# Output weights split and softmax sums inverted inside the attention stage; the first expert's gate and up weights loaded inside the output stage

## The chip, the core and the metric

The kernel runs on one core of a Trainium2 chip. The metric is the device time of that core in microseconds (us), from first to last instruction. The core has five engines, each with a queue of its own: PE (TensorE, matmul), DVE (VectorE, elementwise), ACT (ScalarE, elementwise and activation functions), POOL (GpSimd) and SP (SyncE, here only a DMA issuer). Engines wait for each other by semaphores alone. DMAs are issued by SP, ACT or POOL and run beside the engines.

## What is computed

A cross attention and a layer of routed experts, all in fp32. T = 4 x 1024 tokens, H = 1024 features, 16 heads of 64, 64 experts of which each token takes 8, inner width 384.

```python
q, k, v = proj(layernorm(x), Wq, bq), proj(ctx, Wk, bk), proj(ctx, Wv, bv)
probs = softmax(where(mask, clip(q @ k.T / 8, -50, 50), -50))
ctx = probs @ v                                   # 16 heads side by side: T x 1024
delta = clip(residual_scale, 0, 0.3) * (ctx @ Wo.T + bo)
x = x + layernorm(delta) * gamma + beta
h = layernorm(x)
scores = softmax(h @ gate_weight.T)               # T x 64
topk_w, topk_idx = top_k(scores, 8); topk_w /= sum(topk_w)
y[t] = sum over the 8 experts e of t:  topk_w * ((silu(h[t] @ w_gate[e]) * (h[t] @ w_up[e])) @ w_down[e])
return x + y
```

## The kernel before, in words

The program is a row of stages. Each is a function that opens a block with a program for every engine, and none overlaps another: at a block's end each engine runs a DRAIN and meets the others at a barrier, POOL clears the stage's semaphores, and a second barrier lets the next stage begin (`Scope.clear`, L53 to L56). Between stages everything goes through tensors in HBM (`kst`, `qst`, `vst`, `ctxst`, `sums`, `rsums`, `h2st`, `table`, `dirst`). fp32 products are made from halves: a value is rounded to `hi` (ACT, a cast to fp32r), `lo` is the rest (DVE, a subtraction), and three matmuls (hi x hi, hi x lo, lo x hi) add up in PSUM.

The stages are: projections k, v and q; `attention_pass`; `reciprocal_pass`; `output_pass`; `experts_pass`.

**Attention** (L379). 4 batches of 16 heads, two heads (a pair) per loop step. A head is 8 units, one for each 128 keys, so a pair has 16 (`U`). In a unit PE makes 4 matmuls of scores for the unit three ahead (L478, L479) and 6 of values (L491 to L493). ACT takes the exponential (`exponential`, L516) and rounds it (`high`, L522); DVE clips and masks it (`clip`, L540) and makes the low half (`low`, L545), which PE waits for. Once per head DVE copies the finished context out of PSUM (`context`, L551), in the third unit of the next head. The value matmuls also make each row's softmax sum, unnormalised context and sum come out together in `att_c`. POOL stores both (L448, L451). SP loads K, Q and V of coming heads as their buffers come free.

**Reciprocals** (L586). All 4096 x 16 sums are loaded to one 128 x 512 tile, inverted by DVE (L606) and stored to `rsums`.

**Output** (L620). 32 tiles of 128 tokens. SP loads a tile of the context (`c_raw`) and of the inverses, each broadcast over a head's 64 rows (`r_t`): L702, L705. DVE multiplies them (`divide`, L909), ACT rounds (L866, L886), DVE takes the low half (`context_low`, L913), and PE multiplies with the output weights (L810 to L812, 52 matmuls per tile with the bias). At the start of the stage SP loads the 1024 x 1024 output weights in eight pieces, four buffers deep (L714), ACT and DVE split each piece (L863, L1021), and PE's first product waits for each. POOL meanwhile sets up constants, loads gamma, beta and the router's weights (`consts_in`, L774) and fills `table` (17 DMAs, L778). DVE does not divide tile 1 until `consts_in` is complete. Then come two layer norms (`normalize`), the store of x1 and h, the router (`logits_of`, `route`) and, per tile, eight indirect DMAs by POOL that scatter one (token, weight) record per token and slot to `table` (L787). DVE overwrites a record buffer only when the scatters of two tiles before have landed (L1008). At the end DVE makes a directory of the experts' tile counts and rows, which SP stores to `dirst`.

**Experts** (L1078). Per tile of 128 (token, expert) pairs: SP loads the tile's records by a row number from the directory (L1161), POOL gathers the token rows (L1200), PE transposes them (L1228), ACT and DVE split them, PE multiplies with gate and up (L1251 to L1253) and down (L1238 to L1240), ACT scales by the router's weight and POOL adds the rows to the output. The weights of the next expert are loaded by ACT's queue and split by ACT and DVE within the first tile of the expert in hand. At the start SP issues, in this order, the directory, expert 0's gate, up and down weights (1536 KB each, L1154), and then the first tile's records.

## Time and profile before

| | us |
|---|---|
| median of 3 runs | 7018.12 |
| lowest and highest run | 7014.53 and 7024.12 |
| the profiled execution | 7019.44 |
| its span, first to last instruction | 7017.9 |

| stage | from | to |
|---|---|---|
| projections | 0 | 1188 |
| attention | 1188 | 2396 |
| reciprocals | 2397 | 2405 |
| output | 2406 | 3026 |
| experts | 3026 | 7018 |

PE is busy for 6732.8 us (96% of the span), DVE for 3284.2, ACT for 3004.5 and POOL for 1123.6. The mean granted clock of TensorE is 0.98 of full speed. Times in rows are counted from the span's start. A row of a timeline begins with start and duration; in brackets behind it stands how long the engine had been idle, and what ended that. "PEld" is PE's weight load, "SPq" or "POOLq" an instruction of that engine's sequencer.

### The profile page before, as it was taken

Reading aid. Unit: us, or ns where it says so; the run is one execution under the profiler, and the core shown is the slowest. Engines: PE = TensorE matmul, PEld = TensorE weight load, DVE = VectorE, ACT = ScalarE, POOL = GpSimd, SP = SyncE. Lnnn points to the kernel's source line nnn. Section 1 sums busy time; section 2 is a strip of 40 time slices with the busy share of each in tenths; the row PEclk is TensorE's granted clock in tenths of the full one; section 3 lists DMA queues with packets and bytes.
Section 4 is the critical chain, followed back from the end, with each engine's and each line's share of the span. In section 5 each row is a group of like instructions: output and inputs, shape, how many; then the busy total and the mean of one; then the engine's idle time right before and its main releaser. Section 6 shows DMA issues by size and latency. Waiting matters only on the chain.

```text
span 7017.9 us, 104312 instructions
## 1 busy us (share of the span) xinstructions
PE 6732.8 (96%) x34594; PEld 5959.8 (85%) x34595; DVE 3284.2 (47%) x4163; ACT 3004.5 (43%) x3554; POOL 1123.6 (16%) x1037
## 2 busy tenths in 40 slices
PE   7989899999999699969999999999999999999998
PEld 6778787888888577769999999999999999999998
DVE  3433323999999688834243443332422223333333
ACT  3321222888888544424343443332422333333333
POOL 0000000000000135521111111111111111111111
PEclk9999999999999899979999999999999999999999
DMA  7663454555555477646576676664644556566565
GB/s 226 189 205 135 150 149 111 130 126 132 126 131 126 133 156 151 144 124 181 135 202 163 172 196 158 158 158 105 180 104 105 131 129 159 130 157 156 142 157 150
DMA packets 691794, 1047.60 MB, mean 149 GB/s; under 512 B 260259, under 2 KB 489636, under 8 KB 691718
## 3 DMA queue, kind: packets, MB, share of 16 engines
q0 software_dynamic: 112656, 374.28, 24.1%
q1 hardware_dynamic: 422676, 375.07, 21.5%
q10 hardware_dynamic: 156386, 297.29, 12.3%
q8 instruction: 41, 0.67, 0.0%
q14 instruction: 35, 0.29, 0.0%
HBM read 724.14 MB, written 322.31 MB: 149 GB/s over the span
## 4 chain that ended last, share of the span: by engine, by line
PE 53%; DMA 2%; issue 1%; ACT 0%; DVE 0%; ACTq 0%; SPq 0%; POOLq 0%; DVEq 0%
PE moe_ps_gate L1251 5%; PE moe_ps_gate L1253 5%; PE moe_ps_gate L1252 5%; PE moe_ps_up L1253 5%; PE moe_ps_y L1240 5%; PE moe_ps_up L1251 5%; PE moe_ps_up L1252 5%; PE moe_ps_y L1238 5%; PE moe_ps_y L1239 5%; PE moe_ps_xT L1228 3%; PE moe_ps_hT L1259 1%; DMA out<-moe_y,moe_rec_s 1%; DMA moe_rec_s<-table 1%; DVE moe_gu_lo L1344 0%; ACT moe_y L1289 0%
## 5 line engine op out<-in xcount | busy, mean ns | idle before, releaser
L1251 PE MATMUL moe_ps_gate<-moe_gu_hi,moe_xT_hi 128*128 128x384 f32 x2288 | 793.3, 347 | 24.1 <-DVE moe_gu_lo L1344 21.0
L1354 DVE TENSOR_TENSOR moe_hidden<-moe_silu,moe_ps_up 128x384 f32<-128x384 f32 x286 | 158.5, 554 | 1327.9 <-PE moe_ps_up L1253 1034.0
L1252 PE MATMUL moe_ps_gate<-moe_gu_lo,moe_xT_hi 128*128 128x384 f32 x2288 | 768.9, 336 | 0.0
L1253 PE MATMUL moe_ps_gate<-moe_gu_hi,moe_xT_lo 128*128 128x384 f32 x2288 | 768.5, 336 | 0.0
L1253 PE MATMUL moe_ps_up<-moe_gu_hi,moe_xT_lo 128*128 128x384 f32 x2288 | 765.1, 334 | 0.0
L1252 PE MATMUL moe_ps_up<-moe_gu_lo,moe_xT_hi 128*128 128x384 f32 x2288 | 764.2, 334 | 0.0
L1251 PE MATMUL moe_ps_up<-moe_gu_hi,moe_xT_hi 128*128 128x384 f32 x2288 | 764.2, 334 | 0.0
L1238 PE MATMUL moe_ps_y<-moe_d_hi,moe_hT_hi 128*128 128x512 f32 x1722 | 700.9, 407 | 1.9 <-DVE moe_hT_lo L1359 1.9
L1289 ACT ACTIVATE moe_y<-moe_ps_y,moe_rec_s 128x1024 f32<-128x1024 f32 x287 | 320.7, 1118 | 889.8 <-PE moe_ps_y L1240 514.9
L1208 POOL DMA_INDIRECT out<-moe_y,moe_rec_s x287 | 458.7, 1598 | 1418.6 <-ACT moe_y L1289 1348.2
L1240 PE MATMUL moe_ps_y<-moe_d_hi,moe_hT_lo 128*128 128x512 f32 x1722 | 678.0, 394 | 0.0
L1239 PE MATMUL moe_ps_y<-moe_d_lo,moe_hT_hi 128*128 128x512 f32 x1722 | 670.3, 389 | 0.0
L545 DVE TENSOR_TENSOR att_p_lo<-att_p,att_p_hi 128x1024 fp32r<-128x1024 f32 x512 | 626.7, 1224 | 61.6 <-ACT att_p_hi L522 55.6
L1284 ACT CAST moe_xT_hi<-moe_ps_xT 128x1024 fp32r<-128x1024 f32 x287 | 291.5, 1016 | 796.0 <-PE moe_ps_xT L1228 795.7
L522 ACT CAST att_p_hi<-att_p 128x1024 fp32r<-128x1024 f32 x512 | 539.8, 1054 | 164.3 <-PE att_ps_o L493 164.3
L1359 DVE TENSOR_TENSOR moe_hT_lo<-moe_ps_hT,moe_hT_hi 128x384 fp32r<-128x384 f32 x286 | 159.5, 558 | 931.0 <-ACT moe_hT_hi L1313 930.7
L1200 POOL DMA_INDIRECT moe_tokens<-h2st,moe_rec_g x288 | 283.3, 984 | 1824.1 <-PE moe_ps_xT L1228 1689.2
L516 ACT ACTIVATE att_e<-att_ps_sc 128x1024 f32<-128x1024 f32 x512 | 522.9, 1021 | 10.6 <-PE att_ps_sc L479 10.6
L1348 DVE TENSOR_TENSOR moe_xT_lo<-moe_ps_xT,moe_xT_hi 128x1024 fp32r<-128x1024 f32 x287 | 351.5, 1225 | 315.2 <-ACT moe_xT_hi L1284 315.2
L1251 PEld LDWEIGHTS moe_ps_gate<-moe_gu_hi,moe_xT_hi 128*128 128x128 f32 x2288 | 433.1, 189 | 26.8 <-DVE moe_gu_lo L1344 22.4
L1307 ACT ACTIVATE moe_silu<-moe_ps_gate 128x384 f32<-128x384 f32 x286 | 141.0, 493 | 693.2 <-PE moe_ps_gate L1253 401.9
L1252 PEld LDWEIGHTS moe_ps_gate<-moe_gu_lo,moe_xT_hi 128*128 128x128 f32 x2288 | 434.1, 190 | 0.0
(223 smaller groups left out, 14244.1 us busy)
## 6 DMA issues: line engine op xcount, KB each, us to landing
moe_raw_g<-in_w_gate ACTq DMA_DIRECT2D x63, 1536.0 KB, 7.1
moe_raw_u<-in_w_up ACTq DMA_DIRECT2D x63, 1536.0 KB, 12.0
moe_raw_d<-in_w_down ACTq DMA_DIRECT2D x63, 1536.0 KB, 6.8
vst<-proj_v_o SPq DMA_DIRECT2D x64, 512.0 KB, 2.6
att_kt<-kst SPq DMA_DIRECT2D x64, 512.0 KB, 3.6
att_qh<-qst SPq DMA_DIRECT2D x128, 256.0 KB, 4.7
att_ql<-qst SPq DMA_DIRECT2D x128, 256.0 KB, 5.5
att_v<-vst SPq DMA_DIRECT2D x128, 256.0 KB, 3.4
```

What stands on the lines that cost most here:

```text
L516: nc.scalar.activation(e32[:, u % 2], sc[:, u % 2], ACT.Exp, scale=1.0 / math.sqrt(HD)).then_inc(exp_done, 1)
L522: nc.scalar.copy(p_hi[:, u % 2], p32[:, u % 2]).then_inc(hi_done, 1)
L545: nc.vector.tensor_tensor(p_lo[:, u % 2], p32[:, u % 2], f32(p_hi[:, u % 2]), ALU.subtract).then_inc(lo_done, 1)
L1208: nc.gpsimd.indirect_dma_start(out=acc[:, :], out_offset=bass.IndirectOffsetOnAxis(ap=rec_s[:].bitcast(I32)[:, 0:1], axis=0), in_=y[:], in ...
L1238: nc.tensor.matmul(y_ps[:, cols], hT_hi[:, c], d_hi[:, b, c, cols], start=(c == 0), stop=False)
L1239: nc.tensor.matmul(y_ps[:, cols], hT_hi[:, c], d_lo[:, b, c, cols], start=False, stop=False)
L1240: last = nc.tensor.matmul(y_ps[:, cols], hT_lo[:, c], d_hi[:, b, c, cols], start=False, stop=(c == CI - 1))
L1251: nc.tensor.matmul(o[:, 0:I], xT_hi[:, c], gu_hi[:, b, k, c], start=(c == 0), stop=False)
L1252: nc.tensor.matmul(o[:, 0:I], xT_hi[:, c], gu_lo[:, b, k, c], start=False, stop=False)
L1253: last = nc.tensor.matmul(o[:, 0:I], xT_lo[:, c], gu_hi[:, b, k, c], start=False, stop=(c == C - 1))
L1289: nc.scalar.activation(y[:], y_ps[:], ACT.Copy, scale=rec_s[:, 1:2]).then_inc(y_done, 1)
L1348: nc.vector.tensor_tensor(xT_lo[:], xT_ps[:], f32(xT_hi[:]), ALU.subtract).then_inc(xT_lo_done, 1)
```

## The change

- **Attention.** The output weights are loaded at the start of the attention stage, right behind the loads of the first pair (L466, L467), 3 MB into a tile `raw` that the experts stage later uses for gate and up weights, and 1 MB into `w_rest`. In batch 1 (`SPLIT_AT`), whose loop over pairs is written out, ACT rounds a 128 x 256 piece in every fourth unit (`weight_high`) and DVE takes its low half two units later (`weight_low`): 32 pieces. `wo_hi` and `wo_lo` outlive the stage.
- **Context stores** move from POOL to SP (`store_context`), between SP's loads of coming heads.
- **Sums.** `sums` and `rsums` are laid out by 128-token tile. When a batch is stored, POOL loads its sums, DVE inverts them (128 x 128) in the last pair of the next batch, and POOL stores the inverses. The last batch's are inverted at the start of the output stage. `reciprocal_pass` is gone.
- **First tiles.** Near the end of attention SP loads x, context and inverses of tiles 0 and 1.
- **Output stage.** It finds the weights split. SP loads expert 0's gate and up weights there (L777). The directory stays in SBUF (`dir_sb`): the three columns are copied into it, not to HBM. The zero rows are written from a 128 x 128 tile in 16 DMAs, formerly 2. `normed` is merged into `scaled`.
- **Experts stage.** SP's first DMA is record 0, whose row is fixed (`REGION`), then the down weights. `tokens_high` and `tokens_low` of tile 0 stand between the split of gate and that of up. POOL clears one of the zero tiles, after the first gather.

```diff
 def attention_pass(...)
+                sp.dma_start(w_first, woT[0:CR * P, :].rearrange("(c p) n -> p c n", p=P)).then_inc(w_in, 16)
+                sp.dma_start(w_rest[:], woT[CR * P:H, :].rearrange("(c p) n -> p c n", p=P)).then_inc(w_in, 16)
+                def store_context(i, bt, b):
+                    sp.wait_ge(c_done, bt * NH + 2 * i + b + 1)
+                    sp.dma_start(ctxst[bass.ds((2 * i + b) * HD, HD), bt * S:(bt + 1) * S],
+                                 c32[b * HD:(b + 1) * HD, b]).then_inc(stored[b], 16)
+                    ...
+                def load(i, bt, i_before, bt_before):
+                    for b in range(2):
+                        bh = bt * NH + 2 * i + b
+                        sp.wait_ge(scores_done, (bh - 1) * C)
+                        load_scores(i, bt, b)
+                        sp.wait_ge(values_done, (bh - 1) * C)
+                        load_values(i, bt, b)
+                        store_context(i_before, bt_before, b)
+                for b in range(2):
+                    sp.dma_start(x_t[:, b], x[b * P:(b + 1) * P, :]).then_inc(first_in, 16)
+                    sp.dma_start(c_raw[:, b], ctx_v[:, :, b * P:(b + 1) * P]).then_inc(first_in, 16)
+                    for k in range(2): ...
+                        sp.dma_start(r_t[k * HD:(k + 1) * HD, b], src).then_inc(first_in, 16)
+                for b in range(2):
+                    store_context(NH // 2 - 1, B - 1, b)
 pool:
-                            pool.dma_start(ctxst[...], c32[...]).then_inc(stored[b], 16)
-                            pool.dma_start(sums[...], c32[...]).then_inc(stored[b], 16)
+                for bt in range(B - 1):
+                    for b in range(2):
+                        pool.wait_ge(stored[b], 32 * (bt + 1) * (NH // 2))
+                    pool.dma_start(sums_t[:], sums[bt * C:(bt + 1) * C]...).then_inc(sums_in, 16)
+                    pool.wait_ge(inverted, bt + 1)
+                    pool.dma_start(rsums[bt * C:(bt + 1) * C]..., rsums_t[:]).then_inc(inverses_stored, 16)
 act, in each unit u of a pair:
+                        if bt == SPLIT_AT and u % WP == 0:
+                            weight_high(i, u // WP)
 dve, in each unit u of a pair:
+                        if bt == SPLIT_AT and u % WP == 2:
+                            weight_low(i, u // WP)
+                        if bt and i == NH // 2 - 1 and u == 5:
+                            invert(bt - 1)
 def output_pass(...)
-                load_context(0, 0)
-                for c in range(C): ...
-                    sp.dma_start(w_raw[:, c % 4], woT[c * P:(c + 1) * P, :]).then_inc(w_in[c % 4], 16)
-                load_context(1, 1)
+                sp.dma_start(sums_t[:], sums[last_batch]...).then_inc(sums_in, 16)
                 sp.wait_ge(cn_done, 1)
                 load_context(2, 0)
+                sp.wait_ge(inverted, 1)
+                sp.dma_start(rsums[last_batch]..., rsums_t[:]).then_inc(inverses_stored, 16)
+                sp.wait_ge(inverses_stored, 16)
+                for raw, src in zip(raw_first, w_first):
+                    sp.dma_start(raw[:], src[0].rearrange("(c p) i -> p c i", p=P)).then_inc(raw_first_in, 16)
 pe:
-                        if first:
-                            pe.wait_ge(w_lo_done, c + 1)
 dve:
+                divide(0, 0)
+                context_low(0, 0)
+                nc.vector.reciprocal(rsums_t[:], sums_t[:]).then_inc(inverted, 1)
 def experts_pass(...)
-                sp.dma_start(dir_sb[:], dirst).then_inc(dir_in, 16)
+                sp.dma_start(rec_g[:], table[REGION:REGION + P, :]).then_inc(rec_g_in, 16)
 act (dve likewise, with tokens_low):
-                split(0, 0, 0, PIECES)
+                split(0, 0, 0, C // 2)
+                tokens_high(0)
+                split(0, 0, C // 2, PIECES)
                 load_gate_up(1)
                 load_down(1)
-                tokens_high(0)
```

How instructions move is shown at three places. The first is DVE inside attention, around the copy of a finished head's context (`att_c`). Before, in the loop over pairs:

```order
L540 TENSOR_SCALAR att_p<-att_e,att_upper 128x1024
L545 TENSOR_TENSOR att_p_lo<-att_p,att_p_hi 128x1024
L549 ISA
L550 REGISTER_ALU
L551 COPY att_c<-att_ps_o 128x1024
L537 REGISTER_ALU
L540 TENSOR_SCALAR att_p<-att_e,att_upper 128x1024
L545 TENSOR_TENSOR att_p_lo<-att_p,att_p_hi 128x1024
```

And now, in batch 1:

```order
L594 TENSOR_SCALAR att_p<-att_e,att_upper 128x1024
L599 TENSOR_TENSOR att_p_lo<-att_p,att_p_hi 128x1024
L605 COPY att_c<-att_ps_o 128x1024
L627 TENSOR_TENSOR ahead_wo_lo<-first_raw,ahead_wo_hi 128x256
L594 TENSOR_SCALAR att_p<-att_e,att_upper 128x1024
L599 TENSOR_TENSOR att_p_lo<-att_p,att_p_hi 128x1024
```

The weight piece stands directly behind the context copy, in units 2 and 10 of a pair; the pieces of units 6 and 14 stand alone.

The second is SP from the end of the attention stage into the output stage. Before (POOL stores the context, so SP has nothing to do at the end of attention):

```order
L598 DMA rec_t<-sums 128x512
L600 DMA rsums<-rec_r 128x512
L595 UNCONDITIONAL_BRANCH
L698 UNCONDITIONAL_BRANCH
L702 DMA out_c_raw<-ctxst 128x8x128
L705 DMA out_r_t<-rsums 64x8x128 x2
L714 DMA out_w_raw<-in_woT 128x1024 x8
L702 DMA out_c_raw<-ctxst 128x8x128
```

And now (`first_raw` is the tile that the expert weights use):

```order
L447 DMA ctxst<-att_c 64x1024
L450 DMA sums<-att_c 8x1x128
L423 UNCONDITIONAL_BRANCH
L743 UNCONDITIONAL_BRANCH
L758 DMA out_sums_t<-sums 128x128
L747 DMA ahead_c_raw<-ctxst 128x8x128
L750 DMA ahead_r_t<-rsums 64x8x128 x2
L762 DMA rsums<-out_rsums_t 128x128
L777 DMA first_raw<-in_w_gate 128x8x384
L777 DMA first_raw<-in_w_up 128x8x384
```

The weight loads have left the stage's start, and the last context store stands in front of the barrier on SP.

The third is SP at the start of the experts stage. Before:

```order
L1152 DMA moe_dir<-dirst 1x514
L1154 DMA moe_raw_g<-in_w_gate 128x8x384
L1154 DMA moe_raw_u<-in_w_up 128x8x384
L1154 DMA moe_raw_d<-in_w_down 128x3x1024
L1156 TENSOR_LOAD moe_dir
L1156 ISA x2
L1160 TENSOR_LOAD moe_dir
L1160 ISA x2
L1161 ISA
L1161 DMA moe_rec_g<-table 128x2
```

And now:

```order
L1189 DMA moe_rec_g<-table 128x2
L1192 DMA moe_raw_d<-in_w_down 128x3x1024
L1193 TENSOR_LOAD first_dir
```

The first record went from behind four DMAs to the front of the queue.

## Rows read from the trace of the kernel before

**Rows 1.** The page: busy tenths of PE in 40 slices of 175 us

```profile
PE   7989899999999699969999999999999999999998
```

**Rows 2.** Windows over the first handover: length, busy by engine, PEclk, DMA share, GB/s

```profile
2380.25:2405.63 25.38, 0.00 (x0) 0.00 (x0) 4.58 (x2) 0.00 (x0) 1.04 (x2) 0.55 0.11 31
2405.63:2456.01 50.38, 21.49 (x52) 13.92 (x53) 15.93 (x18) 12.62 (x13) 14.94 (x34) 0.58 0.78 254
```

**Rows 3.** Timeline from the end of attention to tile 2 of the output stage

```profile
2379.85 0.40 PE L493 MATMUL att_ps_o<-att_p_hi,att_v 128*128 128x512 f32 x1
...
2396.73 0.35 SPq L598 DMA_DIRECT2D rec_t<-sums  x1
...
2405.63 0.39 SPq L702 DMA_DIRECT2D out_c_raw<-ctxst  x1
...
2409.61 0.91 POOL L774 DMA_DIRECT2D out_gate<-in_gateT  x1
...
2424.49 1.22 DVE L909 TENSOR_TENSOR out_cn<-out_c_raw,out_r_t 128x1024 f32<-128x1024 f32 x1
...
2428.10 0.80 PE L810 MATMUL out_ps_o<-out_w_hi,out_c_hi 128*128 128x512 f32 x1 [47.85 <-DVE out_c_lo L913]
...
2433.86 0.51 PE L810 MATMUL out_ps_o<-out_w_hi,out_c_hi 128*128 128x512 f32 x1 [0.28 <-DVE out_w_lo L1021]
...
2452.33 1.23 DVE L909 TENSOR_TENSOR out_cn<-out_c_raw,out_r_t 128x1024 f32<-128x1024 f32 x1 [8.43 <-DMA out_r_t<-rsums]
...
2456.01 0.50 PE L810 MATMUL out_ps_o<-out_w_hi,out_c_hi 128*128 128x512 f32 x1 [1.61 <-DVE out_c_lo L913]
...
2471.15 1.71 PE L822 MATMUL out_ps_tps<-out_ident,out_h 128*128 128x128 f32 x8 [2.47 <-ACT out_h L892]
```

**Rows 4.** Source line L413, the attention block's end: durations in ns, start

```profile
L413 POOLq DRAIN x1: 10517/10517/10517, 2385.5 to 2385.5; - x1
```

**Rows 5.** DMA issues by line: KB each, median us to landing

```profile
ctxst<-att_c POOLq DMA_DIRECT2D x64, 256.0 KB, 2.8
out_r_t<-rsums SPq DMA_DIRECT2D x64, 256.0 KB, 12.4
out_gate<-in_gateT POOLq DMA_DIRECT2D x1, 256.0 KB, 19.8
```

**Rows 6.** Waits in attention from 1300 to 2370 us: total, times, longest

```profile
ACT att_p_hi L522 <- PE att_ps_o L493: 149.8, 463, 0.6
...
PEld att_ps_o L491 <- DVE att_p_lo L545: 21.6, 58, 0.4
```

**Rows 7.** Timeline, DVE's inversion of all sums

```profile
2399.40 3.35 DVE L606 RECIPROCAL rec_r<-rec_t 128x512 f32<-128x512 f32 x1 [17.89 <-DMA rec_t<-sums]
```

**Rows 8.** Windows, the first loads of the attention stage

```profile
1190.00:1200.00 10.00, 2.44 (x6) 1.98 (x7) 1.10 (x5) 0.35 (x1) 0.00 (x0) 0.50 1.09 259
```

**Rows 9.** Timeline of SP, the first load for the second pair

```profile
1214.22 0.36 SPq L424 DMA_DIRECT2D att_kt<-kst  x1
```

**Rows 10.** Timeline of the start of the experts stage

```profile
3026.75 0.38 SPq L1154 DMA_DIRECT2D moe_raw_g<-in_w_gate  x1
...
3031.11 31.94 SPq L1161 DMA_DIRECT2D moe_rec_g<-table  x3
...
3034.69 3.56 DVE L1344 TENSOR_TENSOR moe_gu_lo<-moe_raw_g,moe_gu_hi 128x768 fp32r<-128x768 f32 x4 [0.69 <-ACT moe_gu_hi L1280]
...
3042.79 1.01 POOL L1200 DMA_INDIRECT moe_tokens<-h2st,moe_rec_g  x1 [15.67 <-DMA moe_rec_g<-table]
...
3050.42 1.94 PE L1228 MATMUL moe_ps_xT<-moe_ident,moe_tokens 128*128 128x128 f32 x8 [47.63 <-DMA moe_tokens<-h2st,moe_rec_g]
...
3054.80 0.68 PE L1251 MATMUL moe_ps_gate<-moe_gu_hi,moe_xT_hi 128*128 128x384 f32 x1 [2.44 <-DVE moe_xT_lo L1348]
```

**Rows 11.** Source line L901, once per tile: durations in ns, first and last start

```profile
L901 ACT ACTIVATE out_d<-out_ps_o,out_rs x32: 1094/1099/1122, 2454.6 to 2974.8; 128x1024 f32<-128x1024 f32 x32
```

**Rows 12.** Waits in the output stage from 2500 to 2980 us: total, times, longest

```profile
DVE out_record L1008 <- DMA table<-out_record,out_slot: 46.2, 16, 5.0
```

More of the change, by code:

```diff
@@ L498, in _, with body @@
                     scores(0, u)
-                def body(pair, bt, next_bt, first):
+                def body(pair, bt, next_bt, first, i=None):
                     for u in range(U):
@@ L524, in _, with weight_high, body @@
                 exponential(0, 0)
-                def body(pair, bt, next_bt, first):
+                def weight_high(c, k):
+                    if c == 0 and k == 0:
+                        act.wait_ge(w_in, 32)
+                    cols = slice(k * WCOL, (k + 1) * WCOL)
+                    nc.scalar.copy(wo_hi[:, c, cols], w_raw[c][:, cols]).then_inc(w_hi_done, 1)
+                def body(pair, bt, next_bt, first, i=None):
                     for u in range(U):
@@ L1212, in _ @@
                 gather(0)
+                nc.gpsimd.memset(f32(d_lo[:, 1]), 0.0).then_inc(zeroed, 1)
                 gather(1)
```

225 lines of the change are left out of this document (112 added, 113 removed).

## Prediction

> **What bounds the kernel now.** I read the page first. PE is busy 96% of the span and sets the end; in 40 slices it shows a handful of places below 9 tenths [rows 1], of which this change touches two: 2275 to 2450 us, from attention to output, and 2975 to 3150 us, from output to experts. The windows are next [rows 2]: between 2380.25 and 2405.63 PE does nothing, and in the 50.4 us after it does 52 matmuls at a mean granted clock of 0.58. At the second place PE's idle time before its first transposes is 47.63 us [rows 10]. Everything else of the experts stage, 3963 us from 3054.80 on, is unchanged code, so what counts is how much sooner PE reaches two marks: the transposes of tile 0 at 2471.15 [rows 3], from where the output stage goes on as before, and the first gate matmul at 3054.80 [rows 10]. Then the timelines show what each waited for, and the waits in attention what the added work can disturb.
>
> **The handover to output, before.** The last value matmul starts at 2379.85 and ends at 2380.25 [rows 3]. The reciprocals' load is issued at 2396.73. Line L413 tells why so late: POOL, which stored the last context, starts its DRAIN at 2385.5 and needs 10.5 us for it [rows 4]; all others stood at the barrier. The reciprocal stage takes until 2405.63. There PE waits for context and weights until 2428.10, and its first product crawls behind the split of the weights. Product 1 waits for `divide` of tile 1 (2452.33, itself waiting for a load) and starts at 2456.01.
>
> **The same, after.** The context copy ends 1.3 us after the last matmul (2381.5; the copy took 1.22 us). SP, with no DRAIN to speak of, issues the two stores by about 2382.3; a landing of 2.8 us as on POOL's queue [rows 5] gives 2385.0. From the end of POOL's DRAIN (2396.0) to the next stage's first issue (2396.73) was 0.7 us, so the output stage begins near 2385.6, 20.0 us sooner. This needs POOL's DRAIN to be hidden. POOL's last DMA is now the store of batch 2's inverses, released in unit 5 of the last pair, ten units of 2.3 us before the end; 10.5 us fit in. The Trainium skill, VectorE: DVE Perf Modes, section The DRAIN you can't avoid, says in my words that the DRAINs of a program's frame take about 12 ns on any engine. By that rule moving the stores off POOL would bring nothing of these 10.5 us and the sum would be 6973; the trace does not agree (10,517 ns), and the row is used.
>
> In the stage, `divide` of tile 0 is first; from `divide` to the first matmul it took 3.6 us (2424.49 to 2428.10), so PE starts at 2389.2 with all weights split. The clock is at its lower level then: a mean of 0.55 over the 25.38 us of rows 2 is 0.5 with some 2.5 us at full speed, so it fell about 2.5 us after the last matmul, and 9 us pass here. The first 13 matmuls took 5.8 us before they turned short (2428.10 to 2433.86). Product 1 ran from 2456.01 to about 2468.7 (the transposes at 2471.15 had waited 2.47), 0.24 us per matmul; the other 39 take 9.4 us. Product 0 ends at 2404.4. Under it lie the last inversion, the bias's low half and the masks, each about 1 us on an engine that waits.
>
> Product 1 needs `divide` of tile 1, and DVE does not pass `consts_in` before it. POOL issues the router's weights 4.0 us into the stage (2409.61). They landed after 19.8 us [rows 5], beside 4 MB of output weights that are gone now. The nearest short transfer on that side is 2.8 us. I take 14, nearer to the row of the thing itself since gamma, beta and 17 fills stay in front or beside: `divide` at 2385.6 + 4.0 + 14 = 2403.6, and product 1 follows 3.7 us later (2452.33 to 2456.01), at 2407.3. PE has then idled 2.9 us, longer than those 2.5, so it starts cold and takes 5.8 + 9.4 = 15.2 us: the transposes stand at 2422.5. The wait for tile 2's inverses falls away, since that load starts 1 us into the stage and takes some 12.4 us [rows 5], and so does the wait of 2.47 us in front of the transposes. Gain to this mark: 2471.15 - 2422.5 = 48.6 us. Ends: consts after 2.8 us let product 1 follow product 0 warm and gain 6 more; after 19.8 us, 6 less. Expert 0's 3 MB stand on SP's queue in front of tile 3's load; at the 259 GB/s of rows 8 they take 12 us, begin behind the inverses' store, near 2399 to 2402, and are over before tile 3's quotient is due near 2425. Cost 0, up to 4 us if they are slow.
>
> **From there to the stage's end.** From tile 0 to tile 31 are 31 steps of 16.8 us (2454.6 to 2974.8, [rows 11]). Of this 1.5 us each is DVE waiting for POOL's scatters to land, 16 times, 46.2 us in all [rows 12]; without them a tile takes 15.3. Nothing of this loop changes. The 14 more DMAs for the zero rows stand on POOL before its first scatter, which must wait for tile 0's router anyway. I take 0, with 12 us to either side, since a landing time is not fixed.
>
> **Inside attention.** The 1070 us of rows 6 hold 58 heads, or 464 units of 2.3 us. ACT idles 0.32 us per unit waiting for PE (149.8 us, [rows 6]); a piece of 128 x 256 costs it about 0.33 us, once in four units: no loss. DVE's pieces cost about 0.33 us: 768 columns took 0.89 [rows 10] and 1024 took 1.22 [rows 3], 1.2 ns per column, and a little on top. PE waits for DVE once per head, after the context copy (58 waits in 58 heads, [rows 6]); a piece directly behind that copy is late by its whole length, in units 6 and 14 it fits in the slack. So 16 x 0.33 = 5.3 us. Ends: 0, or all 32 pieces on both engines, 21 us. Three inversions of 128 x 128, a quarter of 3.35 us [rows 7], 0.9 us each, come three units after a copy, and slack takes more than half: 1.2 us. SP's load of 4.2 MB at the start takes 16 us at the 259 GB/s that the queue moved there [rows 8], from 1206 at the latest to 1222; pair 1's K is issued at 1214.22 [rows 9] and needed 8 units later, at 1232. Hidden; 5 us at worst. The unrolled batch: the Trainium skill, Runtime: NRT & Kernel Launch, section Instruction fetch mechanics, says that straight code is fetched ahead at next to no cost and a taken branch may stall. By that rule seven back edges go and a little is won; the trace has PE at 9 in every slice inside attention, back edges included [rows 1], so the sum has 0. Attention costs 6.5 us in all.
>
> **The handover to experts.** The stage begins near 3026.5 at the old count. Record 0 was issued at 3031.11 behind the 4.6 MB of weights that began at 3026.75 and POOL could gather only at 3042.79 [rows 10]. Now it is first: 2 us, POOL at 3028.7. From gather to transposes took 7.6 us (to 3050.42): 3036.3. From there to the first gate matmul 4.4 us: 3040.7, a gain of 14.1 us. DVE must have gate's low halves by then: before, with one memset more and the weights still to arrive, it had them at 3038.3. Up is split behind the tokens, by 3040.7 + 3.6 = 3044.3, and PE wants it 24 matmuls of 0.24 us after 3040.7, at 3046.5: 2.2 us to spare. Expert 1's weights are issued later, measured from PE's start, than before; they are split inside tile 0, whose later steps they can delay: 0 taken, 5 us at worst. If the gather starts later than 3028.7, each us is lost whole.
>
> **Sum.** -48.6 + 6.5 - 14.1 = -56.2 us against the profiled 7019.44 (span 7017.9): 6963.2. The median of the runs, 7018.1, lies 1.3 lower. Forecast 6962.
>
> **Rivals.** (a) The output stage eats part of it. If every tile needs 18.2 us instead of 16.8, because scatters land later, 31 steps cost 43 us: 7005. For it: the loop is bound by a landing time in half of its tiles. Against: the traffic beside it is unchanged. Chance 0.07. (b) DVE and ACT are fuller than I think and all 32 pieces stand in PE's way, 15 us more, or POOL's DRAIN is exposed after all (10.5 us): 6973 to 6978. For it: DVE already makes PE wait once per head [rows 6]. Chance 0.13. (c) The gain is larger: constants land early and the tile loop has fewer scatter waits, 6 + 15 us: 6941. Chance 0.10. (d) The change does not do what it says: the early loads are there, but product 0 or the first expert tile still waits for a load, and only the reciprocal stage and the DRAIN are saved, 20 us: 6998. The split is complete 500 us ahead by the order of the code, so 0.03. (e) Slower: SP now waits for the context copy (`c_done`) between two heads' loads, and K and Q stand behind it. Decisive is whether they land within the 8 units, 18.4 us, from their issue to their use. The slowest load of rows 5 on SP's queue took 12.4 us, and the store adds some 0.9 us of issue and 2.8 of landing: 2 us are left even then. Were each of 62 heads late by 2 us, that is +124: 7086; the point of no gain is 0.9 us per head. Nothing in the trace comes near it: 0.03.
>
> **Chances.** Forecast, within 10 us: 0.64. The 8-in-10 range reaches to (b) and (c) and half way to (d): 6944 to 6984. 0.2% is 14 us, about what a measurement of this kernel can tell from no change. Faster by more: 0.94 (the forecast, b, c, d and part of a); within: 0.03 (the bad end of a); slower: 0.03 (e).
>
> **What would show it.** The output stage's first PE matmul about 9 us after the last of attention instead of 48; no DRAIN of 10 us of POOL between them; PE waiting for DVE in units 2 and 10 of batch 1 by some 0.3 us more; product 1 waiting on `divide` of tile 1, and that on POOL's constants; the gather of tile 0 about 2 us into the experts stage. Wrong would be: PE waiting for K or Q inside attention, or tiles of the output stage longer than 17.5 us on average.

## The result, and the profile of the changed kernel

The changed kernel took 6939.98 us (median of 4 runs, 6924.79 to 6941.96), the kernel before 7021.12 (median of 4, 7014.53 to 7029.08): a ratio of 0.9876, with a 95% interval of 0.9864 to 0.9887. The forecast was 6962, with a range of 6944 to 6984. The sign was right and the time missed the range: 81 us were gained where 56 were expected. The profiled execution took 6939.49 us, its span 6937.4. Of all executions below one stands apart: one of e6's four took 13739 us, about twice the time of the others, and is left out of what is said of e6.

The page again has PE in 40 slices. Of the two 6s of [rows 1] the first, at the handover to output, is a 9 now, and at the handover to the experts (17th and 18th slice) stand 8 and 9.

```profile
PE   7989898999999999899999999999999999999998
```

The windows answer to [rows 2]: length, busy time of PE, PEld, DVE, ACT and POOL, granted clock, DMA share, GB/s. The first goes from 0.5 us before the end of the last value matmul (2385.54) to the output stage, the second from there to the transposes of tile 0.

```profile
2385.04:2390.95 5.91, 0.50 (x3) 0.06 (x1) 1.22 (x1) 0.00 (x0) 0.00 (x0) 0.83 0.21 45
2390.95:2422.14 31.19, 27.53 (x105) 20.59 (x106) 16.50 (x24) 8.44 (x9) 21.75 (x48) 0.87 0.87 291
```

From the end of the last value matmul to the output stage it is now 5.4 us instead of 25.4, and in the next 31 us PE does 105 matmuls (before: 52 in 50 us). The timeline of this stretch answers to [rows 3]:

```profile
2390.99 1.23 DVE L949 TENSOR_TENSOR out_cn<-ahead_c_raw,ahead_r_t 128x1024 f32<-128x1024 f32 x1 [4.19 <-SPq L756]
...
2394.25 0.91 POOL L819 DMA_DIRECT2D out_gate<-in_gateT  x1
...
2394.61 0.80 PE L854 MATMUL out_ps_o<-ahead_wo_hi,out_c_hi 128*128 128x512 f32 x1 [9.07 <-DVE out_c_lo L953]
...
2404.04 1.23 DVE L949 TENSOR_TENSOR out_cn<-ahead_c_raw,ahead_r_t 128x1024 f32<-128x1024 f32 x1 [7.13 <-issue]
...
2422.04 1.09 PE L866 MATMUL out_ps_tps<-out_ident,out_h 128*128 128x128 f32 x8
```

PE starts 3.6 us behind the start of the first quotient (`divide`), as forecast, after 9.07 us idle instead of 47.85. The quotient of tile 1 begins at 2404.04, with PE still in the second half of product 0, so product 1 follows without a wait. The transposes of tile 0 stand at 2422.04, 49.1 us sooner than before. Line L423, the attention block's end, shows POOL's DRAIN [rows 4] short and early:

```profile
L423 POOLq DRAIN  x1: 546/546/546, 2368.7 to 2368.7; - x1
```

Of the loads, the router's weights (KB, us to landing) answer to [rows 5], and so does the second line, from the view of the tile `r_t` (least, median and most us to landing):

```profile
out_gate<-in_gateT POOLq DMA_DIRECT2D x1, 256.0 KB, 9.7
```

```profile
DMA to landing us min/median/max: 6.2/7.5/8.8
```

They were 19.8 and 12.4 us. That the inverses (`r_t`) land sooner was not forecast. The tile loop shows it too. First the eviction (ACT's copy of a product out of PSUM), once per tile [rows 11], then DVE's wait for scatters from 2440 to 2920 us [rows 12]:

```profile
L941 ACT ACTIVATE out_d<-out_ps_o,out_rs x32: 1098/1119/1119, 2409.5 to 2904.4; 128x1024 f32<-128x1024 f32 x32
```

```profile
DVE out_record L1048 <- DMA table<-out_record,out_slot: 0.2, 1, 0.2
```

31 steps take 494.9 us instead of 520.2, and of 46.2 us of waits for scatters 0.2 are left (2.0 in the whole stage). The waits in attention, from 1300 to 2370 us as in [rows 6]:

```profile
ACT att_p_hi L568 <- PE att_ps_o L539: 142.2, 438, 0.6
...
PEld att_ps_o L537 <- DVE att_p_lo L599: 26.9, 58, 0.7
```

PEld waits for DVE as often as before (58 times), 5.3 us longer in all, and PE and PEld never for K or Q. The start of the experts answers to [rows 10]:

```profile
2953.98 0.35 SPq L1189 DMA_DIRECT2D moe_rec_g<-table  x1
...
2956.61 1.00 POOL L1235 DMA_INDIRECT moe_tokens<-h2st,moe_rec_g  x1 [1.97 <-DMA moe_rec_g<-table]
...
2962.44 1.94 PE L1263 MATMUL moe_ps_xT<-moe_ident,moe_tokens 128*128 128x128 f32 x8 [30.00 <-DMA moe_tokens<-h2st,moe_rec_g]
...
2966.82 0.68 PE L1286 MATMUL moe_ps_gate<-moe_gu_hi,moe_xT_hi 128*128 128x384 f32 x1 [2.44 <-DVE moe_xT_lo L1384]
```

Put together, from mark to mark of the two profiled executions:

```
stretch                                          before    after   change   forecast
attention, first to last exponential             1173.4   1178.0     +4.6       +6.5
last exponential to output's first instruction     32.6     12.6    -20.0      -20.0
from there to tile 0's transposes                  65.5     31.1    -34.4      -28.6
from there to eviction 31                         503.6    482.4    -21.2          0
eviction 31 to first gate matmul                   80.0     62.4    -17.6      -14.1
first to last gate matmul                        3933.0   3939.9     +6.9          0
```

(The forecast's -28.6 is its 48.6 less the 20.0 of the line above.) The fourth line is the miss; the others are within 7 us. It is less than the 25.3 us between the two evictions, since tile 0's eviction came 12.5 us before its transposes here and 16.5 before. Of the last, the changed kernel's own three profiles have 3937.4, 3939.9 and 3943.1 us, the kernel before and its variants (e2, e12, e13) 3933.0 to 3936.7. So most of the 6.9 us is what executions differ by; whether the rest belongs to the change stays open.

### The profile page after: what moved, and what is told of

Same layout as the page of the kernel before. It is cut to its first block, busy times and chain, and to the rows that moved or that the text cites. A ratio compares the mean times of both kernels' runs of the same rounds, so it can differ in the third digit from the quotient of the medians.

```text
span 6937.4 us, 103787 instructions
## 1 busy us (share of the span) xinstructions
PE 6721.4 (97%) x34594; PEld 5953.2 (86%) x34595; DVE 3281.9 (47%) x4189; ACT 3009.0 (43%) x3578; POOL 1064.6 (15%) x930
## 3 DMA queue, kind: packets, MB, share of 16 engines
q10 hardware_dynamic: 156386, 297.29, 12.4%
## 4 chain that ended last, share of the span: by engine, by line
PE 52%; DMA 3%; issue 1%; ACT 1%; DVE 0%; SPq 0%; ACTq 0%; POOLq 0%; DVEq 0%
PE moe_ps_gate L1286 5%; PE moe_ps_gate L1287 5%; PE moe_ps_gate L1288 5%; PE moe_ps_up L1288 5%; PE moe_ps_up L1286 5%; PE moe_ps_up L1287 5%; PE moe_ps_y L1275 5%; PE moe_ps_y L1273 5%; PE moe_ps_y L1274 5%; PE moe_ps_xT L1263 3%; DMA out<-moe_y,moe_rec_s 2%; DMA moe_rec_s<-table 1%; PE moe_ps_hT L1294 1%; ACT moe_y L1325 0%; DVE moe_gu_lo L1380 0%
## 5 line engine op out<-in xcount | busy, mean ns | idle before, releaser
L1380 DVE TENSOR_TENSOR moe_gu_lo<-first_raw,moe_gu_hi 128x768 fp32r<-128x768 f32 x512 | 455.7, 952 | 9.8 <-ACT moe_gu_hi L1316 9.4
```

What stands on the lines that cost most here:

```text
L1380: nc.vector.tensor_tensor(low, raw, f32(high), ALU.subtract).then_inc(w_lo_done, 1)
```

## Experiments

Ratios are to the kernel before on the same chip. Runs of one group share a chip. The changed kernel had 0.9876 above, 0.9893 in the group of e5 to e8 and 0.9861 in that of e9 to e12. The loop is measured from eviction 0 to 31: 520.2 us before, 494.9 in the changed kernel's first profile. The kernel before has this one profile, of an execution of 7019.44 us. Its median was 7021.5 us beside e9 to e12, but 7005.1 beside e1 to e4 and 7005.5 beside e5 to e8; there its loop was not profiled, and differences from 520.2 may be too large by a part of those 16 us.

### Where the waits for scatters went: e1, e2, e3, e12

One part of the change had no term in the forecast: the sums' inverses changed from one row of T columns per head, 16,384 bytes from row to row, to a layout by tile, where the 16 rows of a tile are 512 bytes apart. `r_t` reads 16 rows of 512 bytes per tile, each into 64 partitions. Theory L says that the distance made this read slow, and everything on the DMA engines with it.

How a late scatter reaches PE is seen in the timeline of the kernel before:

```profile
2557.91 0.23 DVE L1008 TENSOR_SCALAR out_record<-out_e,out_rsum 128x8 f32<-128x8 f32 x1 [3.19 <-DMA table<-out_record,out_slot]
...
2569.75 1.34 PE L822 MATMUL out_ps_tps<-out_ident,out_h 128*128 128x128 f32 x8 [2.27 <-ACT out_h L892]
2570.74 0.78 PE L810 MATMUL out_ps_o<-out_w_hi,out_c_hi 128*128 128x512 f32 x1
2571.31 0.63 PE L811 MATMUL out_ps_o<-out_w_lo,out_c_hi 128*128 128x512 f32 x1
```

DVE waits 3.19 us for the scatters, so its layer norm is late, and PE idles 2.27 us before the transposes. Then its clock is at the lower level: matmuls of 0.63 us follow each other every 0.43 us, for some 3 us, instead of every 0.23. This wait is paid for twice. Not every one is: after pauses of 1.09, 1.40, 1.63 and 1.89 us before the transposes of other tiles the matmuls came every 0.23 us at once.

**e1** puts the inverses back and nothing else (shown are the tensor and the loop's load; the stores and the first tiles' loads follow it):

```diff
-rsums = scratch("rsums", (T // P, NH, P))
+rsums = scratch("rsums", (NH, T))
-src = rsums[bass.ds(i, 1)].rearrange("o (c k) n -> k c (o n)", k=2)[k].partition_broadcast(HD)
+src = rsums.rearrange("(c k) t -> k c t", k=2)[k, :, bass.ds(i * P, P)].partition_broadcast(HD)
```

> The changed kernel with one thing undone: the inverses of the sums lie again as one row of T columns per head (512 bytes per read, 16 KB apart) instead of by tile (16 rows of 512 bytes, 8 KB in one piece); the sums themselves, and all else, stay as changed. Theory L (the layout of the inverses made their broadcast reads quicker, so that the scatters land sooner and VectorE no longer waits for them): the loads of r_t land after about 12.4 us instead of 7.5, the DMA share of the tile loop rises from 0.62 to about 0.73, VectorE waits some 46 us for scatters again, and the 31 steps from output eviction 0 to 31 take about 520 us instead of 494.9: 6940 + 25 = 6965 us. Rival P (the scatter waits went for another reason: where the tensors lie, the phase in which the loop begins, fewer tiles in SBUF): the loop keeps 495 us, and the kernel 6940 +-5 us.

Measured: 6951.52 us, ratio 0.9921 (0.9904 to 0.9937). The loop took 508.7 us. The wait for scatters:

```profile
DVE out_record L1048 <- DMA table<-out_record,out_slot: 32.3, 15, 4.9
```

The waits are back, though 14 us short of the 46.2 of before, and `r_t` lands after 12.6 us. The loop is 14 us longer than in the changed kernel's first profile and 25 us longer than in its fastest (483.6, e5, on another chip). **e2** does the opposite, to the kernel before; only the read and the reciprocal stage's store differ:

```diff
-sp.dma_start(dst, r[:]).then_inc(stored, 16)
+for h in range(sums.shape[0]):
+    sp.dma_start(rsums[:, h].rearrange("(k j) n -> k j n", k=K), r[h * K:(h + 1) * K].rearrange("p (j n) -> p j n", n=P)).then_inc(stored, 16)
```

> The kernel before with one thing done: the inverses are stored by tile (the reciprocal stage writes them with 16 small transfers instead of one, which may cost that stage 5 to 10 us, to be read from its own trace), and the output stage reads them so. Theory L: the loop from output eviction 0 to 31 takes about 495 us instead of 520.2, r_t lands after about 7.5 us instead of 12.4; the kernel takes 7021 - 25 + 5 to 10 = about 7001 to 7006 us. Rival P: the loop keeps 520 us, and the kernel takes 7026 to 7031 us.

Measured: 6992.39 us, ratio 0.9980 (0.9971 to 0.9990), with 11.86 us for the issue of the 16 stores, which put the output stage 11.3 us later. The loop took 490.0 us instead of 520.2. **e3** is e1 with rows 128 columns longer, `scratch("rsums", (NH, T + P))`:

> As e1_inverses_by_head, but each head's row of inverses is 128 columns longer, so the rows lie 16,896 bytes apart instead of 16,384. If it is the power of two in the distance that makes the reads slow, the loop is at 495 us and the kernel at 6940; if it is only that the 16 pieces are not in one stretch, it is like e1 by theory L (520 us, 6965). By rival P both are at 6940.

Measured: 6952.44 us, ratio 0.9928 (0.9912 to 0.9945). `r_t` lands after 7.8 us and the waits for scatters are gone (1.9 us), so it is the distance and not that the pieces lie apart; but the loop took 507.8 us. Why is told below (e15). **e12** puts the same 128 columns into the kernel before. Two lines:

```diff
-ctxst, sums, rsums = scratch("ctxst", (H, T)), scratch("sums", (NH, T)), scratch("rsums", (NH, T))
+ctxst, sums, rsums = scratch("ctxst", (H, T)), scratch("sums", (NH, T)), scratch("rsums", (NH, T + P))
-dst = rsums.rearrange("h (k n) -> (h k) n", n=n)
+dst = rsums[:, 0:sums.shape[1]].rearrange("h (k n) -> h k n", n=n)
```

> The kernel before with one thing changed: each head's row of inverses is 128 columns longer, as in e3. Nothing else is touched; the reciprocal stage writes them with one transfer as before. Theory L (the distance of 16,384 bytes alone makes the scatter waits): the loop from output eviction 0 to 31 takes 490 to 500 us instead of 520, the constants land after about 12.5 us instead of 19.8, and the kernel takes 25 to 30 us less than before: a ratio of 0.9957 to 0.9964. Rival (the distance matters only with the other parts of the change in place): a ratio above 0.999.

Measured: 6978.36 us, ratio 0.9938 (0.9925 to 0.9952): 43 us of the 96 that the whole change brought on this chip. In its profile, in this order: the eviction of L901, one window of the loop, landing of `r_t` and of the router's weights, and the wait for scatters.

```profile
L901 ACT ACTIVATE out_d<-out_ps_o,out_rs x32: 1117/1119/1120, 2446.4 to 2929.9; 128x1024 f32<-128x1024 f32 x32
```

```profile
2500.00:2900.00 400.00, 400.00 (x2035) 318.32 (x2035) 359.89 (x796) 199.25 (x257) 209.37 (x203) 1.00 0.65 168
```

```profile
out_r_t<-rsums SPq DMA_DIRECT2D x50, 256.0 KB, 6.3
```

```profile
out_gate<-in_gateT POOLq DMA_DIRECT2D x1, 256.0 KB, 12.4
```

```profile
DVE out_record L1008 <- DMA table<-out_record,out_slot: 1.9, 1, 1.9
```

The same window of the kernel before, and below it of the changed kernel:

```profile
2500.00:2900.00 400.00, 381.62 (x1893) 302.69 (x1892) 331.72 (x731) 182.35 (x238) 199.06 (x189) 0.97 0.77 155
```

```profile
2500.00:2900.00 400.00, 397.43 (x1997) 315.25 (x1996) 350.25 (x767) 192.13 (x246) 207.17 (x200) 0.99 0.62 156
```

With 512 bytes more from row to row, the engines move more (168 GB/s for 155) in less of their time (0.65 for 0.77), scatters land after 3.5 us instead of 8.8 (medians), PE is never idle and its clock stays at 1.00. The loop takes 483.5 us: 29 steps of 15.71 us and two shorter ones, with no idle time of PE left to lose in the window. Theory L stands, from both sides. The change's own loop was even 11 us longer than that.

The Trainium skill, DMA: Bandwidth & Descriptors, section Latency and other measured facts, has a row on this: copies whose rows lie large powers of two apart lose rate, from 207 GB/s at 512 KiB to 103 at 4 MiB, and at 4 MiB a pad of 4 KiB restores it while one of 192 bytes does not. Our 16 KiB is far below its range and our pad of 512 bytes was enough, so measurement and page agree only in kind; what in the memory does it, no run here shows.

**e11** tests how far this goes. It is e10 (below) with the stored context's rows longer too, `scratch("ctxst", (H, T + P))`.

> e10 with the stored context's rows 128 columns longer (16,896 bytes apart instead of 16,384), as e3 had it for the inverses. The output stage reads it in pieces of 512 bytes at that distance. Theory L extended (any read of small pieces at a distance of 16,384 bytes is slow): c_raw lands sooner than the 5.0 to 6.6 us of the runs with the inverses by tile, by 1 us or more, and the DMA share of the loop falls from 0.62; the time of the kernel stays, since the loop has no scatter waits left to lose. Rival (it is the broadcast, 64 partitions reading one row, that makes the distance matter): c_raw lands as before, share 0.62.

Measured: 6918.97 us, ratio 0.9856 (0.9841 to 0.9872), beside e10's 0.9865 (0.9850 to 0.9880). `c_raw` landed after 5.6 us instead of 5.7, with a DMA share from 2440 to 2920 us of 0.60 instead of 0.62. So these reads of 512 bytes, 16,384 bytes apart, do not suffer where each partition has its own row; the read that did is the one in which 64 partitions share each row. That the sharing makes the difference is the likeliest reading, but the two reads also differ in the number of rows (1024 and 16).

### What was left in the loop: e15

**e15** is e3 once more, in another group.

> e3 again, on another chip and beside others. If the stalls of TensorE at its logits' matmuls (0.7 us in each turn of the loop, followed by some 3.4 us at the lower clock) belong to this kernel, the loop takes about 508 us again; if they belong to the execution, it takes 484 to 496 us, and the ratio falls to 0.987 to 0.989.

Measured: 6961.09 us, ratio 0.9913 (0.9897 to 0.9930), and 514.7 us for the loop. The stalls came again, so they are not chance of one execution. They stand at the logits' matmuls or right behind them, in nearly every turn of the loop:

```profile
2716.86 1.50 PE L876 MATMUL out_ps_lps<-out_gate,out_h2T 128*128 128x64 f32 x12
2718.86 0.22 PE L876 MATMUL out_ps_lps<-out_gate,out_h2T 128*128 128x64 f32 x1 [0.50 <-issue]
2719.59 0.52 PE L876 MATMUL out_ps_lps<-out_gate,out_h2T 128*128 128x64 f32 x3 [0.51 <-issue]
2719.87 0.78 PE L854 MATMUL out_ps_o<-ahead_wo_hi,out_c_hi 128*128 128x512 f32 x1
2720.44 0.63 PE L855 MATMUL out_ps_o<-ahead_wo_lo,out_c_hi 128*128 128x512 f32 x1
```

PE waits twice for about 0.5 us for nothing that the profile names, and here too low-clock matmuls follow. The turn of two tiles costs 34 us instead of 31.4. The changed kernel had three steps of this kind (18.8, 19.1 and 20.3 us) in its first profile and none in e5's, whose loop took 483.6 us. Why e3 stalls in most turns and the changed kernel only now and then stays open. The loop's own instructions don't decide it: e13 (below) has e12's output stage word for word, and where e12's steps are 15.7 us, about every second one of e13 takes 15.8 to 18.2 (489.2 us for the loop). The two ran on different chips, so whether the chip or the code ahead of the loop makes the difference is not separated.

### Attention: e4, e10

**e4** moves DVE's pieces of the weights one unit forward, away from the context copies:

```diff
-                        if bt == SPLIT_AT and u % WP == 2:
+                        if bt == SPLIT_AT and u % WP == 1:
                             weight_low(i, u // WP)
```

> The changed kernel with the low parts of the output weights' pieces computed by VectorE in units 1, 5, 9 and 13 of a pair instead of 2, 6, 10 and 14, so that none stands right behind a context copy. The prediction put 16 x 0.33 = 5.3 us of the attention stage's cost on just these places; the stage (first to last exponential) took 4.6 us longer than before. Theory of the prediction: it now takes 0 to 1 us longer than before, and the kernel gains 4 to 5 us: 6935. Rival (each of the 32 pieces costs a little wherever it stands, or the cost is that of the loop written out): it still takes 4 to 5 us longer, and the kernel stays at 6940.

Measured: 6924.31 us, ratio 0.9885 (0.9868 to 0.9901). First and last exponential in the changed kernel, then in e4:

```profile
1200.32 1.02 ACT L562 ACTIVATE att_e<-att_ps_sc 128x1024 f32<-128x1024 f32 x1 [10.30 <-PE att_ps_sc L525]
...
2378.34 1.02 ACT L562 ACTIVATE att_e<-att_ps_sc 128x1024 f32<-128x1024 f32 x1
```

```profile
1202.64 1.02 ACT L562 ACTIVATE att_e<-att_ps_sc 128x1024 f32<-128x1024 f32 x1 [9.90 <-PE att_ps_sc L525]
...
2376.05 1.02 ACT L562 ACTIVATE att_e<-att_ps_sc 128x1024 f32<-128x1024 f32 x1
```

1178.0 and 1173.4 us. The latter is the kernel before's own number (1199.6 to 2373.0): ACT's 32 pieces, the batch written out and the inversions cost nothing, nor do DVE's pieces where they stand now. **e10** is e4 again, beside **e9**, the changed kernel:

> The changed kernel as it is, as the measure for the two that follow it: a ratio of 0.988 to 0.989 to the kernel before, and an attention stage 4.6 us longer (first to last exponential) than with the pieces moved.

> The changed kernel with the low parts of the weight pieces in units 1, 5, 9 and 13 of a pair, as in e4, now beside the changed kernel on one chip. The attention stage took 1173.4 us with it instead of 1178.0. Theory: nothing later gives this back, so it is 4 to 5 us faster than e9. Rival: the output stage or the experts give it back, and the two are within 2 us.

Measured: 6925.95 (e9) and 6924.70 us (e10), ratios 0.9861 (0.9845 to 0.9876) and 0.9865 (0.9850 to 0.9880). In attention e10 again took 1173.5 us and e9 1178.6, so the mechanism holds; in the whole time 5 us can't be told from the spread of 16 us between runs of one kernel. No version here is shown to be faster than the changed one.

### The start of the output stage: e5, e6

> The changed kernel as it is, as the measure for the others of this group. Its ratio to the kernel before should be 0.988 again, its loop from output eviction 0 to 31 take 488 to 496 us, its attention stage 4.6 to 5 us longer (first to last exponential) than the 1173.4 us of before.

**e5**, the unchanged measure: 6928.58 us, ratio 0.9893, loop 483.6 us. **e6** issues expert 0's weights first (their old place, behind tile 2's load, falls away):

```diff
+                for raw, src in zip(raw_first, w_first):
+                    sp.dma_start(raw[:], src[0].rearrange("(c p) i -> p c i", p=P)).then_inc(raw_first_in, 16)
                 for b in range(2):
                     sp.sem_inc(c_in[b], 48)
```

> The changed kernel with the 3 MB of expert 0's gate and up weights issued as the first transfers of the output stage, ahead of everything else, instead of after the third tile's context. Theory C (the constants landed after 9.7 us instead of 19.8 because no weights are on their way at that time): gate lands after 17 to 22 us again, product 1 can't follow product 0, the step from output eviction 0 to 1 is about 20 to 24 us instead of 12.6, and the kernel takes about 8 to 12 us more than the changed one. Rival (their landing has to do with POOL's own issues, not with what else is in flight): gate lands after about 10 us, and the time doesn't move.

Measured: 6937.18 us (median of three; 6939.89 with the execution of 13739 us), ratio 0.9908 (0.9888 to 0.9927). That is 8.6 us more than e5. The ratios' intervals overlap, but each of the three is slower than all four of e5, and from the stage's first instruction to tile 0's transposes the profiles have 45.2 us instead of 31.0. The size was about as theory C had it, and the reason was not: gate landed after 10.5 us, and the step from eviction 0 to 1 stayed at 12.6. What was late stood on the same queue:

```profile
2389.94 2.23 SPq L760 DMA_DIRECT2D out_sums_t<-sums  x1
...
2409.06 0.95 DVE L1058 RECIPROCAL out_rsums_t<-out_sums_t 128x128 f32<-128x128 f32 x1 [15.69 <-DMA out_sums_t<-sums]
...
2411.20 0.79 PE L860 MATMUL out_ps_o<-out_bo_hi,out_ones_row 1*128 1x512 f32 x1 [10.18 <-DVE out_bo_lo L1062]
```

The 64 KB of sums came behind 3 MB on SP's queue, DVE stood at the inversion, and the bias's low half, behind it, held product 0. The early landing of the constants has two parts. With the old distance but all the rest of the change (e1) gate lands after 12.5 us, with the new distance or layout but nothing else of the change (e12 and e2) after 12.4 and 12.5, with neither after 19.8, with both after 9.7. So the distance is one part. That the other is the 4 MB of output weights is argued and not shown: e1 differs from the kernel before in all else too, and in e6, with 3 MB of weights issued just ahead, gate landed after 10.5 us for e5's 9.9.

### GpSimd's DRAIN: e7, e13, e14

**e7** lets GpSimd issue the context and sum stores again (`pool.dma_start` for `sp.dma_start` in `store_context`; the last pair's behind the loop).

> The changed kernel with the context and sum stores issued by GpSimd again, as before the change, instead of by SyncE. Theory D (GpSimd's drain of 10.5 us at the end of the stage stood on the path of before and is hidden now): the output stage begins about 23 us after the attention's last exponential starts instead of 12.6, and the kernel takes about 10 us more than the changed one. Rival (the drain is short or absent when the transfers before it have landed long ago): 12.6 us, and no more time.

Measured: 6926.14 us, ratio 0.9888 (0.9872 to 0.9905), as in e5. The output stage began 14.2 us after the last exponential instead of 12.6. The rows of POOL's DRAIN at the end of attention in e7, in e13 and in e14:

```profile
L423 POOLq DRAIN  x1: 4220/4220/4220, 2391.4 to 2391.4; - x1
```

```profile
L413 POOLq DRAIN  x1: 10928/10928/10928, 2382.7 to 2382.7; - x1
```

```profile
L423 POOLq DRAIN  x1: 3167/3167/3167, 2394.7 to 2394.7; - x1
```

**e13** takes `pool.wait_ge(stored[b], 32 * NPAIR)` out of e12 and gives it to SyncE; **e14** adds it to e7.

> The padded kernel of before (e12) with GpSimd's last wait, for its own stores to land, done by SyncE instead; GpSimd still issues the stores in its hardware loop. Theory W (the long drain follows the wait): the drain is 3 to 5 us, begins right behind the last issue, and the reciprocal stage begins 8 to 9 us sooner, so a ratio 0.0012 below e12's 0.9938. Theory H (the loop, or the number of transfers issued, makes it long): the drain takes 10.5 us, from about 2.7 us earlier, and the stage begins about 2 to 3 us sooner.

> e7 (the changed kernel with the context and sum stores on GpSimd, the last pair's outside its loop) with a wait of GpSimd for its own stores to land at the end of the stage. Theory W: the drain takes 10.5 us instead of 4.2 and begins 3 us later, so the output stage begins about 9 us later than in e7, and the kernel takes about 9 us more. Theory H: the drain takes 1 to 4 us, and the output stage begins 0 to 3 us later than in e7.

Measured: e13 6982.60 us, ratio 0.9947 (0.9930 to 0.9963); e14 6940.40 us, ratio 0.9887 (0.9870 to 0.9903). Both DRAINs are as theory H has them, and the output stage begins 8.8 us after the start of the last context copy in e14, 7.0 in e7. (The two ran on different chips, and their ratios are the same, 0.9887 and 0.9888. The profiled execution of e14 is 10 us longer, most of it in its loop, 491.2 us for 484.3, with PE's stalls.) The long one comes where the last transfers are issued inside GpSimd's loop, with the wait or without, and a short one where they are issued behind it; in e7 and e14 a store and two waits stand between that loop and the last transfers, so the loop as such is not shown to be the cause. It is not a full rule: the output stage's loop of scatters ends in a DRAIN of 2678 ns in the kernel before.

### The start of the experts: e8

**e8** loads gate and up in the experts stage again, behind record 0.

> The changed kernel with expert 0's gate and up weights loaded at the start of the experts' stage again (behind record 0), instead of in the output stage. The prediction's term for the start of that stage was 14.1 us for weights, record and directory together; the traces give 15.5. If the weights alone carry it, the first gate matmul comes 24 to 28 us after the stage's first instruction instead of 12.8, and the kernel takes 12 to 15 us more than the changed one. If the record's and directory's trips carry it (the gather can start at once now), the weights arrive while the tokens are gathered, and it costs 2 to 6 us.

Measured: 6927.04 us, ratio 0.9893 (0.9876 to 0.9909), as e5. From eviction 31 to the first gate matmul it took 64.4 us (62.4 in e5, 80.0 before). The transposes came 10.4 us into the stage instead of 8.5:

```profile
2940.36 0.34 SPq L1186 DMA_DIRECT2D moe_rec_g<-table  x1
...
2943.00 1.00 POOL L1231 DMA_INDIRECT moe_tokens<-h2st,moe_rec_g  x1 [1.98 <-DMA moe_rec_g<-table]
...
2950.78 1.94 PE L1259 MATMUL moe_ps_xT<-moe_ident,moe_tokens 128*128 128x128 f32 x8 [31.93 <-DMA moe_tokens<-h2st,moe_rec_g]
```

The gather begins 2.6 us into the stage in both, and its tokens reach PE 7.8 us later instead of 5.8. So the early weights bring 1.9 us, by leaving the gather alone. The timelines of [rows 10] and of the changed kernel part the 15.5 us that PE's first gate matmul comes sooner in the stage: record 0 is issued 4.7 us sooner, since four other issues and the reading of the directory no longer stand ahead of it; from its issue to the gather it takes 2.6 us instead of 11.7, since 4.6 MB no longer stand ahead of it on SP's queue; and 1.8 us are the gather's own. The second part, 9.0 us, is the largest, and e8, where the weights follow the record, keeps it.

## Why the prediction was wrong

**The step that failed** is the term for the tile loop, 0: "Nothing of this loop changes. ... I take 0, with 12 us to either side, since a landing time is not fixed." The loop's instructions did not change, but the addresses of one of its loads did, and in the prediction the new layout of the inverses was not priced at all. Rival (a) leaned on the same slip ("the traffic beside it is unchanged"). The rows to see it were there: `r_t`, 256 KB, took 12.4 us to land [rows 5], 4.4 times the store of the same size there, and DVE waited 46.2 us for DMA in the very loop [rows 12]. Measured, the distance alone is worth 36.7 us in the loop (e12) and the layout alone up to 30.2 (e2); the changed kernel's profile kept 25.3 of them, since stalls of PE at its logits' matmuls took some 11. The tile without waits was also put too low: 15.3 us, where the loops without waits settle at 15.7 (e5, e12). Rival (c), 6941 us at 0.10, named this outcome and its time, but as "fewer scatter waits" without a cause. That it hit the time within 1 us is luck: from tile 0's transposes on the loop gave 21.2 us where it had 15, attention and the experts' start were 5.4 us better than forecast, and the experts' matmuls took 6.9 back.

**A term that was mis-sized** is the landing of the constants, 9.7 us where 14 was taken. Of the 10.1 us saved there, the inverses' distance alone (e12) brings 7.4, and the change without it (e1) 7.3. The early landing let product 1 follow product 0 without a pause, at the full clock, and brought 5.8 us more up to tile 0's transposes: about the 6 that the prediction gave as the bound for it.

**What held.** The stage's 20.0 us sooner start is exact, as is PE's first matmul 3.6 us after the quotient; its first 24 took 7.9 us, where the working gives 8.4. The gather stood 2.6 us into the experts stage, where about 2 was said. Attention's cost stood where the working put it: 4.6 us for 6.5, with as many waits as before and each a little longer, and nil when DVE's pieces are moved (e4). A piece took DVE 0.42 us where 0.33 was taken. The extra 1.2 us for inversions and anything for the batch written out were not seen. SP's waits for `c_done`, rival (e), delayed no K or Q.

**Right with a reason too broad.** The 10.5 us of POOL's DRAIN were on the path [rows 4] and are gone. But moving the stores off GpSimd was not what it took: e7 has them there at a cost of 1.6 us. The 12 ns of the Trainium skill that the prediction sets beside this row are stated there for the DRAINs of the runtime's preamble and postamble. A DRAIN at the end of a stage is another, so the 10,517 ns neither bear the page out nor speak against it.

**The experts' start** was 15.5 us sooner from the stage's first instruction instead of 14.1, plus 2.1 us from the tail of the output stage, which had no term: GpSimd's DRAIN there began 4.8 us after its last scatter was issued before, and 2.4 us after it now. It is 2.4 in every run that keeps the directory in SBUF and 2.9 to 4.8 in those that store it (before, e2, e12, e13), but SP was through with that store 5 us before GpSimd (3017.7 and 3022.8 us), so it did not hold the barrier itself; why the scatters land sooner stays open. Of the 15.5 us the gate and up weights in the output stage carry 1.9 (e8), the record's place on the queue 9.0.

## What to carry to other kernels

A change of a tensor's layout in HBM is a change of every loop that reads it: price the read by its landing time against another of its size, and where a small read lands slowly, change the distance of its rows first; here 128 unused columns bought 43 us of 7020 in two lines. A wait of a helper engine on a DMA can cost PE more than its own length: after the pause of 2.27 us above, matmuls came every 0.43 us for some 3 us. Look at what stands behind a load on its own queue: 64 KB behind 3 MB cost the output stage 14 us (e6), and one record of 1 KB behind 4.6 MB held the first gather of the experts for 9.

## What the runs showed of the hardware

- 64 partitions reading the same rows of 512 bytes: 256 KB landed after 12.4 us with the rows 16,384 bytes apart, and after 6.3 with 16,896 (e12). For rows that each partition reads alone, the same step changed nothing (512 KB after 5.7 and 5.6 us, e10 and e11).
- After a pause of PE of 2.27 us, or of twice 0.5 us close together, the matmuls came every 0.43 us instead of every 0.23 for about 3 us (the lower of the clock's two levels, 1.2 GHz). After pauses of 1.09, 1.40, 1.63 and 1.89 us in the same loop of the kernel before they did not, after one of 1.08 us in the changed kernel they did: the length of the pause alone does not tell.
- GpSimd's DRAIN at the end of a stage took 10.5 and 10.9 us behind a loop of stores, 3.2 and 4.2 behind stores outside a loop, and 0.5 where its last transfer was long over.
- Transfers of one queue in line: 64 KB landed after 3.1 us alone and after 19.1 behind 3 MB (e5, e6), and 1 KB took 11.7 us from issue to use behind 4.6 MB, 2.6 ahead of them (the kernel before, e8).
